# One stored transfer per task for the bands, and the loads of k issued by ScalarE

## The chip, the cores and the metric

The kernel runs on one core of a Trainium2 chip. The time is the device time of one launch, in microseconds, and lower is better. Engines are named as in the profile: PE is TensorE, DVE VectorE, ACT ScalarE, POOL GpSimd, SP SyncE, which only issues transfers here.

## The reference

x is 8 tiles of 512 tokens by 128. Each tile goes through half an expert layer, attention, and half an expert layer again, each behind a layer norm:

```python
x = x + 0.5 * ffn(layernorm(x))        # 8 experts, 128 -> 512 -> 128, summed over all experts
x = x + attention(layernorm(x))
x = x + 0.5 * ffn(layernorm(x))
# ffn:  h = silu(x @ wg) * (x @ wu);  acc + h @ wd
# attention, 16 heads of 8: q, k rotated;  rel = rel_emb[clip(j - i, -32, 32) + 32]
scores = q @ k.T / sqrt(8) + einsum(q, rel)          # causal
attn = softmax(scores)
ctx = attn @ v + einsum('bhqk,qkd->bhqd', attn, rel)
out = ctx @ w_o.T
```

The relative term differs from a constant only within 32 positions left of the diagonal, so it is computed on a band: per query 32 probabilities.

## The kernel before

**Passes.** PASSES names 16 expert passes: A of tile t (first expert layer) and B of tile t (second one), of CH = 32 chunks each (8 experts, 4 blocks of 128 hidden units). A chunk n is gate (three matmuls of 512 columns, L814 to L818), tanh on ACT (L965), gated on DVE (L1100), up (three matmuls, L747 to L749), product on DVE (L1106), hi, a cast on ACT (L971), lo, the rest on POOL (L1274), down (L833, L834) and down_lo (L841) on PE. At a pass's end acc copies the sum to xn (L982), sum_turned turns it on PE (L753), sum adds it on DVE (L1155). A layer norm is ln_stats on DVE (L1068, L1073), ln_rstd, four small steps on POOL (L1258 to L1263), ln_scaled on ACT into the same buffer xn (L948), ln_turned on PE (L759), ln_hi on ACT (L995) and ln_lo on DVE (L1078).

**Attention** of a tile runs beside the passes of other tiles, in four groups of four heads, and a group in 11 tasks: one for the first 128 queries (4 heads), two for the second 128 (2 heads each), four each for the third and fourth (1 head). A task is scores on PE (L896), near, largest and shift on DVE (L1203, L1208, L1214), exp on ACT (L1016), p_hi, the f16 part, on ACT (L1027, L1029), and the rest by p_lo on DVE (L1221) or p_lent on POOL (L1289). All of it lies in probs, a ring of PB = 4 buffers: first the high parts of the task's heads, then the low parts. Two kinds of transfers leave from there, both issued by SyncE: p_turn (L712), a DMA transpose into probs_t, for values on PE (L914); and store_band (L697, L700), which writes the last 160 columns to a scratch in memory, from which load_band on ACT's queue (L1055) reads 32 diagonal columns per query. A two-head task takes two store transfers (L697), one for each part, since in the scratch all high parts of four heads come before all low parts. band_turn (L729) transposes the bands, band_values on PE (L923) multiplies by rel_c, once for the high and once for the low parts, outproj (L932) closes the group, and attention_sum (L1245) adds it.

**k and q.** Per tile project (L747 to L749) makes q and k in four steps, rotate turns them on DVE (the last step L1185), qk_hi and qk_lo split them in the buffer rope, qk_store (L666) writes them to memory. load_q (L1035) is one transfer on ACT's queue per group; load_k (L722) is four transfers of 64 KB per group on SyncE's queue, one for each head of k_pad. v_add (L1190) writes v into the low half of rope and so waits until k is stored. load_k waits for the stores of k and for the scores of the group two before.

**Order.** Each engine's program is one list, made while the kernel is built by a planner: `step(engine, takes, time, name, arg, ...)` gives every step an engine, a duration, a wanted time and what it follows; the wanted time is shifted by a table LATER, a number for each kind of step. The planner takes, at every moment, on the engine that can start first, the open step with the earliest start. So a changed table, duration or engine of one step moves steps on all engines.

Of the kernel before, what the change touches and what calls it, by code (L numbers as in the profile page):

```python
# [8 lines left out]
def macaron_kernel(nc, x_d, wg_d, wu_d, wd_d, watt_d, wo_d, rel_g_d, rel_g0_d, rel_c_d, rel_c0_d,  # L9
                   rel_k0_d, rel_v0_d, cos_d, sin_d, window_d, ident_d, lanes_d, out_d):  # L10
    F32 = mybir.dt.float32
    F32R = mybir.dt.float32r
    F16 = mybir.dt.float16
    BF16 = mybir.dt.bfloat16
# [10 lines left out]
    H = 16  # L25
# [21 lines left out]
    VS = 3  # L47
    VD = VS * DH + 2
# [47 lines left out]
    def quad_of(k):  # L96
# [11 lines left out]
    LATER = {"acc": -1137.9, "attention_sum": -218.9, "band_turn": -615.6, "band_values": -1012.4, "constants":  # L108
             913.7, "denominators": 112.4, "down": 37.6, "down_lo": -171.0, "exp0": -214.2, "exp1": -230.3, "exp2": -211.3,
             "exp3": -141.2, "fill": 311.2, "gate": 24.9, "gated": 150.9, "hi": -147.6, "largest0": -149.5, "largest1":  # L110
             -244.5, "largest2": -479.1, "largest3": -133.8, "ln_hi": -663.8, "ln_lo": -640.3, "ln_rstd": 807.9,
             "ln_scaled": -89.2, "ln_stats": -1456.5, "ln_turned": -297.3, "lo": -278.6, "load_band0": -814.8,
# [5 lines left out]
             "p_turn3": 46.7, "prepare_hi": -414.6, "prepare_lo": 27.6, "product": 137.5, "project": -422.1, "project_v":  # L118
             50.0, "qk_hi": -1536.9, "qk_lo": -982.9, "qk_store": -451.6, "qrel": 24.3, "qrel_copy": -357.1, "qrel_store":
# [284 lines left out]
    with ctx:  # L404
# [167 lines left out]
        for k in range(B * NK):  # L572
            counted[k % PB] += 2 if HEADS[TASKS[k % NK][1]] == 2 else 1
            stores.append(16 * counted[k % PB])
# [795 lines left out]
```

## Time and profile before

| | us |
|---|---|
| median of 3 runs | 1328.59 (1327.34 to 1330.45) |
| the profiled execution | 1326.2 |
| its span on the core | 1324.4 |
| PE busy | 1303.8 |
| DVE busy | 1212.5 |
| POOL busy | 1061.2 |
| ACT busy | 1060.4 |

The profile is one execution. Busy times count computing instructions only; an engine's DMA issues, waits and branches don't count, though an issue holds the queue of the engine that makes it. A group of rows of one line gives count, shortest, median and longest duration. A wait is put down to the event that came last.

### The profile page before, as it was taken

What the parts mean: (1) busy time and instruction counts of PE and PEld (TensorE: products, weight loads), DVE (VectorE), ACT (ScalarE), POOL (GpSimd) and SP (SyncE); (2) the same over time, 40 slices, a digit from 0 to 9 for tenths busy, and PEclk for the clock granted to TensorE, in tenths of its full rate; (3) what the DMA queues carried; (4) which work ended last, traced back from release to release, by engine and by line L of the source; (5) the groups of instructions that cost most, each with busy time, mean ns of one, the idle gap of its engine ahead of it and who ended that gap; (6) DMA issues with size and microseconds to landing.
All of it is one profiled execution on the core that took longest, in us unless ns stands there. A gap on an engine that the chain in (4) does not pass through costs nothing. (4 is left out here: it accounts for less than half of the span.)

```text
span 1324.4 us, 28469 instructions
## 1 busy us (share of the span) xinstructions
PE 1303.8 (98%) x8334; PEld 1051.1 (79%) x8334; DVE 1212.5 (92%) x2613; ACT 1060.4 (80%) x2097; POOL 1061.2 (80%) x979
## 2 busy tenths in 40 slices
PE   8999999999999999999999999999999989999998
PEld 6888888777777788878888888887888867888887
DVE  7887999999999999999999999999999989998665
ACT  6765888878888888888887888888888778887565
POOL 7977888879778887887877977889778787788565
PEclk9999999999999999999999999999999999999999
DMA  6404899999999999999999999999999999997100
GB/s 200 154 1 129 150 228 222 200 219 230 202 233 201 196 197 196 248 184 217 203 209 229 193 223 209 190 231 205 208 201 206 188 220 214 203 176 144 13 9 8
DMA packets 718555, 241.39 MB, mean 182 GB/s; under 512 B 652480, under 2 KB 681920, under 8 KB 718400
## 3 DMA queue, kind: packets, MB, share of 16 engines
q1 hardware_dynamic: 562240, 180.84, 69.7%
q10 hardware_dynamic: 156160, 58.74, 22.0%
q8 instruction: 66, 1.08, 0.3%
q14 instruction: 89, 0.73, 0.2%
HBM read 77.33 MB, written 69.86 MB: 111 GB/s over the span
## 5 line engine op out<-in xcount | busy, mean ns | idle before, releaser
L1274 POOL TENSOR_TENSOR hid_lo<-hid,hid_hi 128x512 fp32r<-128x512 f32 x511 | 658.8, 1296 | 190.2 <-ACT hid_hi L971 101.6
L971 ACT CAST hid_hi<-hid 128x512 fp32r<-128x512 f32 x512 | 317.1, 626 | 94.9 <-PE acc L834 56.8
L1100 DVE SCALAR_TENSOR_TENSOR hid<-hid,work 128x512 f32<-128x512 f32 x512 | 344.5, 679 | 44.6 <-ACT hid L965 44.0
L965 ACT ACTIVATE hid<-work 128x512 f32<-128x512 f32 x512 | 305.9, 600 | 96.5 <-PE work L818 62.1
L1106 DVE TENSOR_TENSOR hid<-hid,work 128x512 f32<-128x512 f32 x512 | 345.8, 680 | 21.7 <-PE work L749 19.5
L1289 POOL TENSOR_TENSOR probs<-exps,probs 128x512 f16<-128x512 f32 (+1 forms) x288 | 304.2, 1061 | 45.1 <-ACT probs L1027 44.2
L1208 DVE TENSOR_REDUCE negmax<-work 128x1 f32<-128x384 f32 (+3 forms) x352 | 220.1, 632 | 0.7
L1016 ACT ACTIVATE exps<-work,negmax_shifted 128x512 f32<-128x512 f32 (+2 forms) x320 | 188.3, 602 | 36.8 <-DVE negmax_shifted L1214 26.1
L747 PE MATMUL work<-xt,wu 128*128 128x512 f32 x512 | 204.9, 400 | 4.0 <-DVE rope L1190 1.5
L841 PE MATMUL acc<-hid_lo,wd 128*128 128x512 f32 x512 | 204.9, 406 | 0.1
L833 PE MATMUL acc<-hid_hi,wd 128*128 128x512 f32 x512 | 203.7, 398 | 0.5 <-ACT hid_hi L971 0.5
L814 PE MATMUL work<-xt,wg 128*128 128x512 f32 x512 | 202.7, 396 | 1.3 <-ACT xt L958 0.8
L815 PE MATMUL work<-xt,wg 128*128 128x512 f32 x512 | 200.2, 391 | 0.0
L818 PE MATMUL work<-xt,wg 128*128 128x512 f32 x512 | 200.1, 391 | 0.0
L749 PE MATMUL work<-xt,wu 128*128 128x512 f32 x512 | 200.1, 391 | 0.0
L834 PE MATMUL acc<-hid_hi,wd 128*128 128x512 f32 x512 | 200.0, 391 | 0.0
L748 PE MATMUL work<-xt,wu 128*128 128x512 f32 x512 | 199.9, 390 | 0.0
L1027 ACT ACTIVATE probs<-exps 128x512 f16<-128x512 f32 (+1 forms) x288 | 167.7, 586 | 12.1 <-issue 4.0
L1203 DVE TENSOR_TENSOR work<-work,rel_win 128x160 f32<-128x160 f32 (+2 forms) x352 | 163.2, 471 | 13.3 <-PE work L896 10.9
L896 PE MATMUL work<-k_pad,qq 128*128 128x512 f32 (+1 forms) x352 | 131.6, 384 | 0.3 <-ACT exps L1016 0.2
L747 PEld LDWEIGHTS work<-xt,wu 128*128 128x128 f32 x512 | 96.2, 188 | 29.1 <-DVE hid L1106 2.1
L814 PEld LDWEIGHTS work<-xt,wg 128*128 128x128 f32 x512 | 96.2, 188 | 23.4 <-DVE hid L1100 1.2
(104 smaller groups left out, 1734.9 us busy)
## 6 DMA issues: line engine op xcount, KB each, us to landing
rel_win<-rel_window_scratch ACTq DMA_DIRECT2D x128, 320.0 KB, 4.0
prob_window_scratch<-probs SPq DMA_DIRECT2D x384, 80.0 KB, 3.3
q_scratch<-rope SPq DMA_DIRECT2D x16, 512.0 KB, 4.2
qq<-q_scratch ACTq DMA_DIRECT2D x32, 256.0 KB, 4.0
k_scratch<-rope SPq DMA_DIRECT2D x16, 512.0 KB, 4.5
rel_window_scratch<-g_s SPq DMA_DIRECT2D x32, 256.0 KB, 3.5
k_pad<-k_scratch SPq DMA_DIRECT2D x128, 64.0 KB, 3.8
prob_window_scratch<-probs SPq DMA_DIRECT2D x32, 256.0 KB, 3.8
```

The lines of the kernel that those rows point to most:

```text
L747: pe.matmul(out, w_hi, m_hi, start=start, stop=False)
L814: pe.matmul(bank[:, :], wg[:, HI, e, cols], x_hi, start=True, stop=False)
L815: pe.matmul(bank[:, :], wg[:, LO, e, cols], x_hi, start=False, stop=False)
L833: pe.matmul(acc[:, :], wd[:, HI, e, cols], hid_hi[:, arg % HH, :], start=(k == 0), stop=False)
L841: pe.matmul(acc[:, :], wd[:, HI, e, cols], hid_lo[:, arg % HH, :], start=False, stop=(k == CH - 1)).then_inc(s_dlo, 1)
L965: act.activation(hid[:, arg % HB, :], work[bank_of["gate", arg]][:, :], ACT.Tanh, scale=0.5).then_inc(s_tanh, 1)
L971: act.copy(hid_hi[:, arg % HH, :], hid[:, arg % HB, :]).then_inc(s_hhi, 1)
L1100: dve.scalar_tensor_tensor(out=hid[:, arg % HB, :], in0=hid[:, arg % HB, :], scalar=1.0, in1=work[bank_of["gate", arg]][:, :], op0=ALU.add ...
L1106: dve.tensor_tensor(hid[:, arg % HB, :], hid[:, arg % HB, :], work[bank_of["up", arg]][:, :], ALU.mult).then_inc(s_hid, 1)
L1208: dve.tensor_reduce(negmax[:, place:place + len(places)], heads, AX.X, ALU.min).then_inc(s_max, 1)
L1274: pool.tensor_tensor(hid_lo[:, arg % HH, :], hid[:, arg % HB, :], hid_hi[:, arg % HH, :].bitcast(F32), ALU.subtract).then_inc(s_hlo, 1)
L1289: pool.tensor_tensor(probs[:, arg % PB, cols:2 * cols], exp_of(arg)[:, 0:cols], probs[:, arg % PB, 0:cols], ALU.subtract).then_inc(s_plent, 1)
```

## The change

Three things are changed.

1. In probs and in the scratch the parts are laid out by pairs of heads: for each pair the two high parts, then the two low parts (a one-head task has its high and its low part, as before). The store of a task is then one transfer in all cases. band_values multiplies by pairs in place of parts: rel_c gets two empty slots (6 in place of 4) and each of the two matmuls takes its window of four slots. by_pairs gives p_hi, p_lo and p_lent their views, and values finds its blocks by the new place.
2. load_k is a step of ACT in place of SP; its waits and its four transfers are the same.
3. LATER has other numbers, and the planner's duration of store_band is 0.62 for all.

The buffer for a small marker (settled) moves into lanes, and the function lower_part is renamed restpart.

```diff
     SCALE = 2.0 ** 14
     VS = 3
+    SLOTS = HQ + 2
+    RC = SLOTS * R
...
-            step("SP", 1.8, first - 14, "load_k", gg, ("qk_store", (t, 1)), ("zero", 7),
+            step("ACT", 1.8, first - 14, "load_k", gg, ("qk_store", (t, 1)), ("zero", 7),
...
-            step("SP", 1.2 if HEADS[i] == 2 else 0.62, due[k] + 2.5, "store_band", k, lower(k),
+            step("SP", 0.62, due[k] + 2.5, "store_band", k, lower(k),
...
-             -131.5, "scores3": 23.8, "shift1": -584.8, "shift2": -672.7, "shift3": -980.9, "split_hi": 63.7, "split_lo":
+             -258.7, "scores3": 20.3, "shift1": -386.5, "shift2": -453.1, "shift3": -684.5, "split_hi": -52.3, "split_lo":
...
-        rel_c = sb("rel_c", [P, HQ, R // DH, DH], BF16)
+        rel_c = sb("rel_c", [P, SLOTS, R // DH, DH], BF16)
...
+        def by_pairs(k):
+
+            quad, i, places, keys = task(k)
+            pairs = max(len(places) // 2, 1)
+            both = probs[:, k % PB, 0:2 * len(places) * keys].rearrange("p (u h c) -> p u h c", u=pairs, h=2)
+            whole = exp_of(k)[:, 0:len(places) * keys].rearrange("p (u c) -> p u c", u=pairs)
+            return both[:, :, HI, :], both[:, :, LO, :], whole
...
-                    base = (quad % (2 * NT) * 2 * HQ + places[0]) * TILE + lo
-                    if n == 2:
-                        for part in (HI, LO):
-                            sp.dma_start(bass.AP(pwin_t, base + part * HQ * TILE, [[W, P], [TILE, n], [1, W - lo]]),
-                                         near[:, part, :, :]).then_inc(stored(arg)[0], 16)
-                    else:
-                        sp.dma_start(bass.AP(pwin_t, base, [[W, P], [HQ * TILE // n, 2 * n], [1, W - lo]]),
-                                     near.rearrange("p h n k -> p (h n) k")).then_inc(stored(arg)[0], 16)
+                    first = quad % (2 * NT) * 2 * HQ + places[0] // 2 * 4 + places[0] % 2
+                    sp.dma_start(bass.AP(pwin_t, first * TILE + lo,
+                                         [[W, P], [TILE if n > 1 else 2 * TILE, 2 * n], [1, W - lo]]),
+                                 heads[:, :, keys - W + lo:keys]).then_inc(stored(arg)[0], 16)
...
-                    for part in (HI, LO):
+                    for pair in range(2):
                         done = pe.matmul(ctx_p[:, :].rearrange("p (i q) -> p i q", i=NT),
-                                         rel_c[:, :, :, :].rearrange("p a s d -> p (a s d)"), band_t[:, :, part, :],
-                                         start=False, stop=(part == LO), skip_group_check=True)
+                                         rel_c[:, 2 - 2 * pair:SLOTS - 2 * pair, :, :].rearrange("p a s d -> p (a s d)"),
+                                         band_t[:, :, pair, :], start=False, stop=(pair == 1), skip_group_check=True)
...
+                if name == "load_k":
+                    t, g = arg // HG, arg % HG
+                    act.wait_ge(s_qst[1], 32 * (t + 1))
+                    if arg < 2:
+                        act.wait_ge(s_zero, 8)
+                    else:
+                        act.wait_ge(s_sc, GK * (arg - 1))
+                    for a in range(HQ):
+                        act.dma_start(k_pad[a:P:HQ, arg % 2, a, :].bitcast(F32),
+                                     bass.AP(k_t, t % VB * 4 * P * L + g * L + a * HG * L,
+                                             [[H * L, 4 * DH], [1, L]])).then_inc(s_kld[arg % 2], 16)
```

Three places of the engines' lists show what the new numbers do. Names are tile<-tiles; line numbers are each kernel's own, and in the changed kernel L808 to L812 is gate, L741 to L743 up, L827 and L828 down, L835 down_lo, L927 outproj, L747 sum_turned, L753 ln_turned.

The first place is PE's list at the last hand-over, from the last output projection of attention (L932) to the first gate of the last pass. Before, 30 wide matmuls lie between it and the turn of the norm (the first and the last of them are shown):

```order
4985 L932 MATMUL work<-wo,ctx_s 128x128 x4
4986 L841 MATMUL acc<-hid_lo,wd 128x512
4987 L814 MATMUL work<-xt,wg 128x512
...
5014 L834 MATMUL acc<-hid_hi,wd 128x512
5015 L841 MATMUL acc<-hid_lo,wd 128x512
5016 L759 MATMUL work<-ident,xn 128x128 x4
5017 L833 MATMUL acc<-hid_hi,wd 128x512
5018 L834 MATMUL acc<-hid_hi,wd 128x512
5019 L841 MATMUL acc<-hid_lo,wd 128x512
5020 L833 MATMUL acc<-hid_hi,wd 128x512
5021 L834 MATMUL acc<-hid_hi,wd 128x512
5022 L814 MATMUL work<-xt,wg 128x512
```

In the changed kernel the same stretch is:

```order
4999 L927 MATMUL work<-wo,ctx_s 128x128 x4
5000 L835 MATMUL acc<-hid_lo,wd 128x512
5001 L827 MATMUL acc<-hid_hi,wd 128x512
5002 L828 MATMUL acc<-hid_hi,wd 128x512
5003 L827 MATMUL acc<-hid_hi,wd 128x512
5004 L828 MATMUL acc<-hid_hi,wd 128x512
5005 L835 MATMUL acc<-hid_lo,wd 128x512
5006 L827 MATMUL acc<-hid_hi,wd 128x512
5007 L828 MATMUL acc<-hid_hi,wd 128x512
5008 L835 MATMUL acc<-hid_lo,wd 128x512 x2
5009 L747 MATMUL work<-ident,xn 128x128 x4
5010 L753 MATMUL work<-ident,xn 128x128 x4
5011 L808 MATMUL work<-xt,wg 128x512
```

Ten wide matmuls and the turn of pass 14's sum now lie between the projection and the turn of the norm, and the gate follows the turn at once.

The second place is SyncE's list from the time when the loads of k of tile 7 start. Before:

```order
701 L722 DMA k_pad<-k_scratch 32x512 x4
702 L700 DMA prob_window_scratch<-probs 128x2x160
703 L712 DMA_TRANSPOSE probs_t<-probs 128x6x128
704 L700 DMA prob_window_scratch<-probs 128x2x160
705 L712 DMA_TRANSPOSE probs_t<-probs 128x8x128
706 L722 DMA k_pad<-k_scratch 32x512 x4
...
711 L700 DMA prob_window_scratch<-probs 128x8x128
712 L712 DMA_TRANSPOSE probs_t<-probs 128x8x128
713 L697 DMA prob_window_scratch<-probs 128x2x160 x2
714 L712 DMA_TRANSPOSE probs_t<-probs 128x8x128
715 L697 DMA prob_window_scratch<-probs 128x2x160 x2
```

In the changed kernel, with the store of k of tile 7 (L677) in the middle:

```order
662 L704 DMA prob_window_scratch<-probs 128x2x160
663 L704 DMA prob_window_scratch<-probs 128x8x128
664 L717 DMA_TRANSPOSE probs_t<-probs 128x8x128
665 L677 DMA k_scratch<-rope 128x2x512 x2
666 L689 DMA rel_window_scratch<-g_s 128x4x128
667 L717 DMA_TRANSPOSE probs_t<-probs 128x8x128
668 L704 DMA prob_window_scratch<-probs 128x4x160
669 L717 DMA_TRANSPOSE probs_t<-probs 128x8x128
670 L704 DMA prob_window_scratch<-probs 128x4x160
671 L717 DMA_TRANSPOSE probs_t<-probs 128x8x128
```

The loads of k are gone from the list, and a two-head task has one store of 128x4x160 where it had two of 128x2x160.

The third place is ACT's list where the first load of k of tile 7 is now. Before, the list has there, behind the load of q:

```order
1780 L1035 DMA qq<-q_scratch 128x512
1781 L1016 ACTIVATE exps<-work,negmax_shifted 128x512
1782 L971 CAST hid_hi<-hid 128x512
1783 L1055 DMA bands<-prob_window_scratch 128x8x32
1784 L1027 ACTIVATE probs<-exps 128x512
1785 L965 ACTIVATE hid<-work 128x512
```

In the changed kernel:

```order
1665 L966 CAST hid_hi<-hid 128x512
1666 L1021 ACTIVATE probs<-exps 128x384
1667 L1049 DMA rel_win<-rel_window_scratch 128x640
1668 L1038 DMA k_pad<-k_scratch 32x512 x4
1669 L960 ACTIVATE hid<-work 128x512 x2
1670 L1011 ACTIVATE exps<-work,negmax_shifted 128x384
1671 L966 CAST hid_hi<-hid 128x512
```

Five issues in a row stand ahead of the next tanh (L960).

## Rows read from the trace of the kernel before

**Rows 1.** Busy time, share of the span and instructions of each engine.

```profile
PE 1303.8 (98%) x8334; PEld 1051.1 (79%) x8334; DVE 1212.5 (92%) x2613; ACT 1060.4 (80%) x2097; POOL 1061.2 (80%) x979
```

**Rows 2.** Stretches: length; busy PE, PEld, DVE, ACT, POOL; clock; DMA share; GB/s.

```profile
0.00:50.00 50.00, 44.75 (x195) 36.53 (x196) 37.74 (x74) 34.93 (x64) 42.44 (x40) 1.00 0.61 197
...
250.00:430.00 180.00, 174.54 (x1167) 136.41 (x1165) 170.66 (x381) 148.62 (x300) 145.31 (x138) 1.00 1.10 214
430.00:880.00 450.00, 449.54 (x3036) 363.26 (x3035) 434.40 (x968) 380.71 (x766) 372.00 (x345) 1.00 1.09 208
880.00:1120.00 240.00, 234.68 (x1646) 188.43 (x1645) 229.48 (x514) 199.48 (x402) 195.82 (x185) 1.00 1.07 208
...
1260.00:1324.40 64.40, 60.69 (x268) 49.53 (x266) 39.55 (x61) 35.71 (x60) 38.43 (x30) 1.00 0.02 7
```

**Rows 3.** Waits of PE, 140 to 1245 us: total, times, longest.

```profile
PE ctx_p L914 <- DMA probs_t<-probs: 2.9, 4, 1.8
PE ctx_p L923 <- DMA band_t<-bands: 1.8, 2, 1.0
PE work L747 <- DVE rope L1190: 1.5, 1, 1.5
PE work L747 <- ACT exps L1016: 1.1, 1, 1.1
```

**Rows 4.** DMA issues by line: duration in ns, shortest/median/longest, first and last start.

```profile
L712 SPq DMA_TRANSPOSE probs_t<-probs x352: 1209/1256/4925, 140.7 to 1223.0; - x176
L697 SPq DMA_DIRECT2D prob_window_scratch<-probs x128: 359/484/1555, 142.1 to 1199.9; - x128
L722 SPq DMA_DIRECT2D k_pad<-k_scratch x128: 448/587/2072, 123.0 to 1151.1; - x128
L1035 ACTq DMA_DIRECT2D qq<-q_scratch x32: 326/350/434, 111.0 to 1147.2; - x32
```

**Rows 5.** Timeline of SP, DVE and PE, 381 to 391 us: start, duration.

```profile
381.45 1.04 SPq L666 DMA_DIRECT2D k_scratch<-rope  x2
...
389.76 0.69 DVE L1190 TENSOR_TENSOR rope<-work,rel_v 128x512 f32<-128x512 f32 x1 [2.53 <-DMA k_scratch<-rope]
...
390.51 0.50 PE L747 MATMUL work<-xt,wu 128*128 128x512 f32 x1 [1.54 <-DVE rope L1190]
```

**Rows 6.** Timeline of ACT, SP and PE, 1076 to 1086 us.

```profile
1076.96 0.63 ACT L1027 ACTIVATE probs<-exps 128x512 f16<-128x512 f32 x1 [2.07 <-DMA probs_t<-probs]
...
1076.21 2.45 SPq L722 DMA_DIRECT2D k_pad<-k_scratch  x4
1078.76 0.53 SPq L700 DMA_DIRECT2D prob_window_scratch<-probs  x1
1079.39 1.23 SPq L712 DMA_TRANSPOSE probs_t<-probs  x1
...
1085.88 0.85 PE L914 MATMUL ctx_p<-probs_t,values 128*25 128x128 f16 x48 [1.84 <-DMA probs_t<-probs]
```

**Rows 7.** Timeline of PE, DVE, POOL and ACT, 1243 to 1253 us.

```profile
1243.69 0.40 PE L834 MATMUL acc<-hid_hi,wd 128*128 128x512 f32 x1
1243.92 1.05 PE L932 MATMUL work<-wo,ctx_s 128*128 128x128 f32 x8
1244.73 0.47 PE L841 MATMUL acc<-hid_lo,wd 128*128 128x512 f32 x1
...
1245.02 0.69 DVE L1245 TENSOR_TENSOR x<-work,x 128x512 f32<-128x512 f32 x1 [0.33 <-PE work L932]
...
1248.49 0.20 POOL L1263 TENSOR_TENSOR shift<-mean_neg,rstd 128x4 f32<-128x4 f32 x1
1248.64 1.29 POOL L1274 TENSOR_TENSOR hid_lo<-hid,hid_hi 128x512 fp32r<-128x512 f32 x1
...
1249.71 1.65 ACT L948 ACTIVATE xn<-x,shift,rstd 128x128 f32<-128x128 f32 x4
...
1252.30 0.59 ACT L995 CAST xt<-work 128x512 fp32r<-128x512 f32 x1
```

More of the change, by code:

```diff
@@ L104, in macaron_kernel @@
     LANDS = {"PE": 0.35, "ACT": 0.35, "DVE": 0.35, "POOL": 0.35, "SP": 2.6}
[L108 to L112, printed above, removed]
[5 rows of a table removed]
-             "p_turn3": 46.7, "prepare_hi": -414.6, "prepare_lo": 27.6, "product": 137.5, "project": -422.1, "project_v":
-             50.0, "qk_hi": -1536.9, "qk_lo": -982.9, "qk_store": -451.6, "qrel": 24.3, "qrel_copy": -357.1, "qrel_store":
[3 rows of a table removed]
-             "store_band3": -469.7, "sum": 611.7, "sum_turned": -628.3, "tanh": -270.2, "up": 27.8, "v_add": 678.4,
-             "v_split": -14.5, "values": -612.1, "zero": 1284.8}
+    LATER = {"acc": -1094.5, "attention_sum": -283.2, "band_turn": -812.0, "band_values": -638.2, "constants":
+             868.8, "denominators": 94.4, "down": 40.5, "down_lo": -282.6, "exp0": -235.8, "exp1": -327.3, "exp2": -134.0,
+             "exp3": -89.0, "fill": 634.3, "gate": 24.8, "gated": 153.4, "hi": -141.5, "largest0": -189.7, "largest1":
+             -271.4, "largest2": -570.6, "largest3": -154.1, "ln_hi": -575.5, "ln_lo": -738.8, "ln_rstd": 736.8,
+             "ln_scaled": -86.0, "ln_stats": -1530.5, "ln_turned": -296.9, "lo": -290.8, "load_band0": -897.7,
[5 rows of a table added]
+             "p_turn3": 383.9, "prepare_hi": -585.7, "prepare_lo": -29.1, "product": 95.7, "project": -277.9, "project_v":
+             58.0, "qk_hi": -1705.2, "qk_lo": -829.6, "qk_store": -477.8, "qrel": 31.4, "qrel_copy": -373.9, "qrel_store":
[3 rows of a table added]
+             "store_band3": -576.7, "sum": 697.1, "sum_turned": -679.8, "tanh": -378.9, "up": 28.5, "v_add": 696.4,
+             "v_split": 178.1, "values": -526.5, "zero": 1337.8}
     OF_TASK = ("scores", "near", "largest", "shift", "exp", "p_hi", "p_lo", "p_lent", "p_turn", "store_band")
@@ L451, in macaron_kernel @@
         ident = sb("ident", [P, P])
-        lanes = sb("lanes", [P, 2])
+        lanes = sb("lanes", [P, 3])
         stats = sb("stats", [P, NT, 6])
@@ L1019, in _ @@
                     quad, i, places, keys = task(arg)
-                    cols = len(places) * keys
                     act.wait_ge(s_exp, unit(quad, places[-1]) + 1)
@@ L1286, in _ @@
                     quad, i, places, keys = task(arg)
-                    cols = len(places) * keys
                     pool.wait_ge(s_phi, arg + 1)
-                    pool.tensor_tensor(probs[:, arg % PB, cols:2 * cols], exp_of(arg)[:, 0:cols],
-                                       probs[:, arg % PB, 0:cols], ALU.subtract).then_inc(s_plent, 1)
+                    upper, rest, whole = by_pairs(arg)
+                    pool.tensor_tensor(rest, whole, upper, ALU.subtract).then_inc(s_plent, 1)
                 if name == "v_split":
@@ L1333 @@
         rel_g0[a, :, :, :, a] = rel[0][:, None]
-    rel_c, rel_c0 = np.zeros((HQ, R, HQ, 4, DH), rel.dtype), np.zeros((HQ, R, HQ, 4, DH), rel.dtype)
-    for a in range(HQ):
-        rel_c[a, :, a, 0:3, :] = rel[1:R + 1][:, None, :]
-        rel_c0[a, :, a, 0:3, :] = rel[0]
+    rel_c, rel_c0 = np.zeros((2, 2, R, HQ + 2, 4, DH), rel.dtype), np.zeros((2, 2, R, HQ + 2, 4, DH), rel.dtype)
+    for a in range(2):
+        rel_c[:, a, :, 2 + a, 0:3, :] = rel[1:R + 1][:, None, :]
+        rel_c0[:, a, :, 2 + a, 0:3, :] = rel[0]
     w_o = np.asarray(inputs["L0_attn_w_o"])
```

55 lines of the change are left out of this document (20 added, 35 removed), and 14 rows, old and new, of the table LATER.

## The prediction

> **What bounds the kernel now.** I read the profile in this order. First the busy shares: TensorE (PE) is busy for 1303.8 of 1324.4 us, 98% [rows 1]. A busy PE is no proof that PE sets the end, so the second view is the table of stretches [rows 2]: it says where PE's 20.6 us of idle time lie. They lie in four places: the start (5.25 us), the stretch 250 to 430 us (180.00 - 174.54 = 5.46), the stretch 880 to 1120 us (240.00 - 234.68 = 5.32) and the end (64.40 - 60.69 = 3.71). The 450 us between 430 and 880 lose 0.46 us in all. The granted clock is 1.00 in every row, so the clock plays no part. The same table shows what stands next in line: from 430 to 880 VectorE (DVE) is busy for 434.40 of 450 us (96.5%) and ScalarE (ACT) for 380.71 (85%). So PE's own work sets the time, DVE has almost no room to catch up after a hole, and ACT has some.
>
> Third, the waits of PE in the attention part [rows 3]: transposes that land late (2.9 us), band transposes (1.8), one wait of 1.5 on DVE's L1190 and one of 1.1 on ACT's exp. Fourth, the stretches where they happen. Until 390.51 us PE stands for 1.54 us because DVE stands for 2.53 us: L1190 overwrites the buffer from which k is being stored and waits for that store. The store was issued at 381.45 behind transposes on SyncE's queue [rows 5]. Until 1076.96 ACT stands for 2.07 us waiting for a transpose, and the 1.1 us of PE on ACT's exp follow from it; until 1085.88 PE stands 1.84 us for a transpose that SyncE issued at 1079.39, after a store (1078.76) which itself followed four loads of k (1076.21 to 1078.66) [rows 6]. So the two clusters are delays of SyncE's queue and its transfers, and the change takes work from just this queue.
>
> **What the change can't move.** The matmuls are the same in number and width: band_values still runs two matmuls of 512 columns per group, with another slice of rel_c as weights; scores, values and the expert matmuls keep their shapes. Wide matmuls (512 columns) follow each other at 0.23 us, start to start [rows 7], and will in the changed kernel. Bytes stay too: a two-head task stores the same 160 KB, in one transfer for two. The regrouping by pairs changes the address pattern of p_hi and the low part only for tile 0 of each group (32 tasks, two runs of 256 columns for one of 512); a tenth more of 0.6 us on 32 instructions would be 2 us of ACT, off the path, and I take 0. The longer constants and subtractions happen before 110 us, where PE loses nothing [rows 2]. I take 0 for the start and the end.
>
> **Part 1, SyncE's queue is relieved.** The loads of k leave it: 128 issues x 0.587 us = 75 us. The second store of the 64 two-head tasks goes: 64 x 0.484 = 31 us. Together 106 us of queue time. What stays is mostly 352 transposes x 1.256 = 442 us [rows 4]. A queue that is not the bound gives back only lateness, so the gain is capped by what PE loses in the two clusters: 5.46 + 5.32 = 10.8 us. I don't take all of it. First, part of the lateness is not issue time: the store of k at 381.45 took over 7 us to land [rows 5], and the transfers' bytes stay. Second, the new order puts some consumers closer. Between the last step of k's rotation and L1190 DVE has in the old order 28, 33 and 23 instructions for tiles 2, 3 and 7; in the new one 22, 35 and 27. Tile 3 and tile 7 get more time, tile 2 less, so the wait at L1190 can come back at tile 2. Third, from the last projection of k of tile 7 to its first scores the new PE order has some 9 us more work (32 us for 23, counting 0.23 us per wide matmul), which gives the second cluster more room. Bounds: all 10.8 us gone, or none. I take a bit under half, -5 us (from -10.8 to 0), since of the waits named in [rows 3], 2.9 + 1.8 + 1.5 us are of this kind and each shortens by one or two issues of 0.5 us rather than vanishing.
>
> A rule speaks against this part. What the rows show first: a group's four loads of k hold SyncE for 2.45 us [rows 6], more than any single wait of PE in [rows 3], so issuing is not small here. The Trainium skill (DMA: Bandwidth & Descriptors, section Issuing engines are not separate DMA queues) says that issuing from several engines saves only the sequencer's time, which is "usually small relative to the DMA itself", since all run on the same 16 DMA engines. By it part 1 would be near 0 instead of -5.
>
> **Part 2, ScalarE issues the loads of k.** 32 times four issues in a row stand ahead of ACT's work: what is queued behind them is tanh of the next chunk (L965), the cast L971 and the exp of the next task, and DVE and then PE wait for those. The trace has no such load on ACT. Nearest rows: ACT's own load of q issues in 0.350 us (4 x 0.350 = 1.4 us); the same load on SyncE in 0.587 (4 x 0.587 = 2.35) [rows 4]. The issue runs while ACT's last instruction still computes (about 0.6 us), so the hole is 0.8 to 1.75 us. Its waits (k stored, the scores of two groups before) are satisfied well before where it now stands: in the new order PE has 10 us of work or more between the load of k and the group's first scores. What does a hole of ACT cost PE? The ACT hole of 2.07 us in [rows 6] cost PE the 1.1 us of [rows 3], in a crowded place. From 430 to 880 us ACT stands idle many times and PE loses 0.46 us in all [rows 2]. Bounds: 0 for all 32, or 32 x 0.4 = 13 us. I take +2 us, near the low end, as most of the loads lie in stretches like the latter.
>
> **Part 3, the new order at the last hand-over.** The last pass (B of tile 7) needs the layer norm of tile 7, which needs the last attention output. The order of before keeps 30 wide matmuls between the last L932 and the turn of the norm, and five more before the first gate; PE loses nothing there. In the new order only ten wide matmuls, the turn of pass 14's sum and the turn of the norm stand between, and then the gate. The chain itself, by [rows 7]: L932 ends at about 1244.8 (the next matmul starts at 1244.73); the sum on DVE ends at 1245.71, and after the statistics and POOL's four steps the shift is ready at 1248.69. Then ACT's scaling 1.65 us (in before it came an us late, at 1249.71, as nothing hurried), so 1250.4; the last transposes and the start of the high cast about 0.3 later, 1250.7; the cast 0.59, 1251.3; the gate at 1251.4, which is 6.6 us after L932. PE's work between is 10 x 0.23, twice four turns of 128 columns (2 x 0.4, by the 0.81 us of L932's eight), and 0.1 for the change of form = 3.2 us, and the gate's third matmul waits some 0.3 us more for the low part. That gives 6.6 - 3.2 + 0.3 = 3.7 us. It is more if the low parts of the last three chunks queue on POOL (1.29 us each, ahead of its norm steps and needed for pass 14's sum, which must leave the shared buffer xn before the scaling starts): then up to 4.8. I take +4.2 us (3.6 to 4.8), as the three chunks do stand close together there. The rest of PE's work is the same, so nothing later gives it back.
>
> **Sum.** On the profiled execution (span 1324.4, time 1326.2): -5 + 2 + 4.2 = +1.2 us. The profiled run lies 2.4 us below the median of the three timed runs (1328.59), an ordinary spread of this kernel (1327.34 to 1330.45), so I set the change on the median: 1328.59 + 1.2 = 1329.8 us. A measurement of this kernel can tell about 0.2%, 2.7 us, from no change; so faster means under 1325.9, slower over 1331.3.
>
> **Rivals.**
> - *SyncE's lateness was nearly all of it.* -9 of the 10.8 us, ACT's loads cost 0.5, the hand-over 4.2: -4.3, that is 1324.3 us. For it: both clusters lead back to that queue [rows 5, 6]. Against: the landing times, and 450 us in which the same queue is as full and PE loses nothing. Chance 0.24.
> - *No relief, only the hand-over.* The clusters come from DMA transfers and crowded norms rather than issue; part 1 gives 0.5, ACT costs 1.5, the hand-over 4.2: +5.2, 1333.8 us, slower. It decides from where part 1 is worth under 3.5 us. Chance 0.22. The rule of the Trainium skill quoted above would have it go this way.
> - *ACT's holes reach PE through DVE.* DVE, 96.5% busy, can't catch up: a hole of ACT of over 1 us becomes a hole of DVE, and 32 x 0.3 = 9.6 us of PE, with -4 for part 1 and 4.2: +9.8, 1338.4 us. It decides from about 0.15 us per load. For it: half of ACT's hole of 2.07 us arrived at PE [rows 3, 6]. Against: ACT's 15% of room. Chance 0.14.
> - *The forecast*, relief and costs within 2.7 us of each other: 0.40, with its own range 1326 to 1331.3.
>
> From these: faster 0.25, within 0.2% 0.40, slower 0.35. The range reaches into both neighbours, from 1323 to 1337 us; outside stay the full relief with no cost of ACT, and the worse half of ACT's case.
>
> **What would show it.** Right: a PE wait of 3.6 to 4.8 us in one or two pieces just ahead of the last pass's first gate, at about 1245 to 1255 us, with the chain L932, sum, statistics, POOL, scaling in front of it; SyncE's queue some 100 us emptier; the idle time of PE from 250 to 430 and 880 to 1120 us down from 10.8 to about 6; four DMA issues of 0.35 to 0.6 us each on ACT, followed by an idle ACT of about 1 us, but seldom an idle PE. Wrong: no stall at the hand-over (then the chain is shorter than I add it up); clusters as large as before, or new ones at L1190 of tile 2; idle time of PE spread through 430 to 880 us right behind the loads of k, which would be the third rival.

## The result, and the profile after

The changed kernel takes 1349.5 us (median of 4 runs, 1344.1 to 1353.7) beside 1329.5 us for the kernel before, run on the same chip (1327.3 to 1332.7). The ratio is 1.0152, with a 95% interval from 1.0118 to 1.0186. So it is slower by 20 us, where 1329.8 us was forecast with a range up to 1337. The profiled execution has a span of 1346.4 us where [rows 1] belongs to one of 1324.4: 22.0 us more.

The busy line of the page, which answers to [rows 1]:

```profile
PE 1318.9 (98%) x8334; PEld 1052.4 (78%) x8334; DVE 1215.3 (90%) x2613; ACT 1049.7 (78%) x2097; POOL 1061.1 (79%) x979
```

The instructions are as many as before. PE's busy time is 15 us longer with the same matmuls: it takes in the short delays between one matmul and the next, so most of the loss doesn't show as idle time in it. The stretches, which answer to [rows 2] (same columns):

```profile
250.00:430.00 180.00, 177.53 (x1189) 141.24 (x1188) 169.10 (x377) 146.20 (x297) 143.56 (x135) 1.00 1.06 201
430.00:880.00 450.00, 444.33 (x3012) 351.76 (x3010) 426.70 (x953) 372.18 (x756) 363.68 (x338) 1.00 1.08 206
880.00:1120.00 240.00, 235.44 (x1571) 187.36 (x1560) 226.53 (x497) 193.36 (x392) 191.41 (x179) 0.99 1.03 204
```

PE's idle time from 250 to 430 us fell from 5.46 to 2.47 us, and from 880 to 1120 us from 5.32 to 4.56. But from 430 to 880 us, where it had been 0.46, it is now 5.67, and DVE does less there (426.70 for 434.40). The waits of PE from 140 to 1262 us, which answer to [rows 3], are short and of many kinds; none is over 1.7 us:

```profile
PE work L890 <- ACT exps L1011: 2.4, 3, 1.6
PE ctx_p L909 <- DMA probs_t<-probs: 2.4, 3, 1.2
PE acc L835 <- POOL hid_lo L1274: 1.7, 4, 0.6
PE acc L827 <- ACT hid_hi L966: 1.2, 3, 0.8
PE work L808 <- DVE rope L1192: 1.2, 1, 1.2
```

To see the rest I set the start of every matmul against the sum of the matmuls before it, taken at their usual spacing, and read how far the wall clock had run ahead. The table gives this lag in us, by the work that PE has done so far (left column). The usual spacing is a choice that moves all columns together by a few us, so only differences between them are read. e12, e4 and e9 are experiments that are told below.

| PE's work, us | before | after | e12 | e4 | e9 |
|---|---|---|---|---|---|
| 150 | 9.7 | 12.4 | 12.8 | 10.3 | 9.3 |
| 400 | 25.4 | 26.5 | 26.3 | 24.8 | 28.8 |
| 650 | 32.4 | 39.0 | 36.9 | 36.4 | 36.3 |
| 900 | 39.8 | 54.4 | 49.6 | 48.7 | 52.1 |
| 1200 | 51.8 | 68.7 | 60.0 | 58.5 | 61.7 |
| 1250 | 52.1 | 74.1 | 66.5 | 63.6 | 64.4 |

Up to 400 us of work the changed kernel loses 1.1 us against before (2.7 at the start, of which 1.6 come back). Between 400 and 1200 it loses 15.8 us more than before, a little in most steps of 50 us, and in the one step from 1200 to 1250, the last hand-over, 5.4 us where before loses 0.3.

**The hand-over.** PE, DVE, POOL and ACT in the timeline, which answer to [rows 7] (start, duration, and in brackets the idle time before):

```profile
1266.89 1.05 PE L927 MATMUL work<-wo,ctx_s 128*128 128x128 f32 x8
...
1267.98 0.69 DVE L1245 TENSOR_TENSOR x<-work,x 128x512 f32<-128x512 f32 x1 [1.28 <-PE work L927]
...
1271.07 0.63 PE L747 MATMUL work<-ident,xn 128*128 128x128 f32 x4 [0.78 <-ACT xn L977]
1271.47 0.20 POOL L1263 TENSOR_TENSOR shift<-mean_neg,rstd 128x4 f32<-128x4 f32 x1
...
1271.81 1.65 ACT L943 ACTIVATE xn<-x,shift,rstd 128x128 f32<-128x128 f32 x4 [0.89 <-PE work L747]
...
1272.45 1.39 PE L753 MATMUL work<-ident,xn 128*128 128x128 f32 x4 [0.76 <-ACT xn L943]
...
1274.52 0.72 PE L808 MATMUL work<-xt,wg 128*128 128x512 f32 x1 [0.68 <-ACT xt L990]
1275.03 0.63 PE L809 MATMUL work<-xt,wg 128*128 128x512 f32 x1
1275.46 0.63 PE L812 MATMUL work<-xt,wg 128*128 128x512 f32 x1
...
1278.02 0.41 PE L743 MATMUL work<-xt,wu 128*128 128x512 f32 x1
```

From the end of the projection (L927, about 1267.9) to the gate (1274.52) it is 6.6 us, the figure of the forecast's chain (6.8 if the end is read from the start of the next matmul, 1267.70, as the forecast did), and the ten wide matmuls and two turns don't fill it. Two chains end together here: the norm's shift is ready at 1271.67, and the scaling (L943) starts at 1271.81, when the turn of pass 14's sum (L747, to 1271.70) has also left the buffer xn.

**ScalarE's row of issues.** The line of the loads of k, which answers to L722 in [rows 4], and two of the 32 places where they stand, in ACT's timeline:

```profile
L1038 ACTq DMA_DIRECT2D k_pad<-k_scratch x128: 456/617/1487, 127.4 to 1185.7; - x128
```

```profile
760.14 0.58 ACT L960 ACTIVATE hid<-work 128x512 f32<-128x512 f32 x1
760.72 0.34 ACTq L1027 DMA_DIRECT2D qq<-q_scratch  x1
761.15 2.41 ACTq L1038 DMA_DIRECT2D k_pad<-k_scratch  x4
763.76 0.79 ACTq L1058 DMA_DIRECT2D bands<-prob_window_scratch  x1
764.66 0.62 ACT L966 CAST hid_hi<-hid 128x512 fp32r<-128x512 f32 x1 [3.94 <-DMA prob_window_scratch<-probs]
...
1087.93 3.45 ACTq L1038 DMA_DIRECT2D k_pad<-k_scratch  x4
1091.76 1.09 ACT L960 ACTIVATE hid<-work 128x512 f32<-128x512 f32 x2 [3.67 <-issue]
```

A load issues in 0.617 us. The row of four takes 2.39 to 3.82 us (median 2.50), its first load 0.467 and each later one 0.62 us (medians). In the first place a load of q and one of bands stand beside it, and ACT computes nothing for 3.94 us; in the second the row alone takes 3.45 us, and ACT stands for 3.67. The hole isn't the row's length, though, since ACT's queue can run ahead of its computing. At 208.02 us the whole row issues while instructions that stand ahead of it in the list still compute (L1011 at 208.39 and 208.75, L998 at 209.10, L966 at 209.58), and the hole is 0.63 us:

```profile
208.02 0.47 ACTq L1038 DMA_DIRECT2D k_pad<-k_scratch  x1
...
209.58 0.66 ACT L966 CAST hid_hi<-hid 128x512 fp32r<-128x512 f32 x1
209.81 0.61 ACTq L1038 DMA_DIRECT2D k_pad<-k_scratch  x1
210.88 0.62 ACT L994 CAST rope<-rope 128x512 fp32r<-128x512 f32 x1 [0.63 <-DVE rope L1187]
```

In 16 of the 32 rows at least one such instruction starts within the row. The holes are 0.63 to 3.94 us. DVE and PE behind the row at 1087.93:

```profile
1092.39 1.28 DVE L1103 SCALAR_TENSOR_TENSOR hid<-hid,work 128x512 f32<-128x512 f32 x2 [0.94 <-ACT hid L960]
...
1091.42 0.40 PE L743 MATMUL work<-xt,wu 128*128 128x512 f32 x1
1093.37 0.44 PE L890 MATMUL work<-k_pad,qq 128*128 128x384 f32 x1 [1.55 <-ACT exps L1011]
```

ACT stands, DVE has no tanh to multiply, the next exp comes late, and PE stands for 1.55 us. In most places PE sees only some tenths of this, later. So the candidates are: the length of the row on ACT; the queue that issues it; the order of the lists, which also changed everywhere; and the hand-over.

### The profile page after: what moved, and what is told of

Read it like the earlier page. It is cut to its first block and busy times, and to the rows that moved or that the text cites. A ratio compares the mean times of both kernels' runs of the same rounds, so it can differ in the third digit from the quotient of the medians.

```text
span 1346.4 us, 28405 instructions
## 1 busy us (share of the span) xinstructions
PE 1318.9 (98%) x8334; PEld 1052.4 (78%) x8334; DVE 1215.3 (90%) x2613; ACT 1049.7 (78%) x2097; POOL 1061.1 (79%) x979
## 3 DMA queue, kind: packets, MB, share of 16 engines
q10 hardware_dynamic: 162304, 67.14, 24.8%
## 5 line engine op out<-in xcount | busy, mean ns | idle before, releaser
L960 ACT ACTIVATE hid<-work 128x512 f32<-128x512 f32 x512 | 307.2, 605 | 125.8 <-PE work L812 55.8
L966 ACT CAST hid_hi<-hid 128x512 fp32r<-128x512 f32 x512 | 316.4, 631 | 78.7 <-DVE hid L1109 44.6
L1011 ACT ACTIVATE exps<-work,negmax_shifted 128x512 f32<-128x512 f32 (+2 forms) x320 | 187.7, 609 | 36.4 <-DVE negmax_shifted L1216 23.1
L808 PE MATMUL work<-xt,wg 128*128 128x512 f32 x512 | 206.0, 402 | 4.4 <-DVE rope L1192 1.2
L835 PE MATMUL acc<-hid_lo,wd 128*128 128x512 f32 x512 | 207.3, 412 | 1.8 <-POOL hid_lo L1274 1.7
L827 PE MATMUL acc<-hid_hi,wd 128*128 128x512 f32 x512 | 204.3, 399 | 2.2 <-ACT hid_hi L966 1.2
L741 PE MATMUL work<-xt,wu 128*128 128x512 f32 x512 | 204.8, 400 | 1.4 <-DVE hid L1109 0.7
L812 PE MATMUL work<-xt,wg 128*128 128x512 f32 x512 | 201.3, 393 | 0.0
L743 PE MATMUL work<-xt,wu 128*128 128x512 f32 x512 | 200.7, 392 | 0.0
L828 PE MATMUL acc<-hid_hi,wd 128*128 128x512 f32 x512 | 199.9, 390 | 0.0
L1021 ACT ACTIVATE probs<-exps 128x512 f16<-128x512 f32 (+1 forms) x288 | 166.6, 588 | 14.1 <-DMA prob_window_scratch<-probs 4.3
L808 PEld LDWEIGHTS work<-xt,wg 128*128 128x128 f32 x512 | 97.0, 189 | 30.1 <-DVE hid L1103 3.9
L741 PEld LDWEIGHTS work<-xt,wu 128*128 128x128 f32 x512 | 96.6, 189 | 27.4 <-DVE hid L1109 3.9
```

What stands on the lines that cost most here:

```text
L741: pe.matmul(out, w_hi, m_hi, start=start, stop=False)
L808: pe.matmul(bank[:, :], wg[:, HI, e, cols], x_hi, start=True, stop=False)
L812: pe.matmul(bank[:, :], wg[:, HI, e, cols], x_lo, start=False, stop=True).then_inc(s_gate, 1)
L827: pe.matmul(acc[:, :], wd[:, HI, e, cols], hid_hi[:, arg % HH, :], start=(k == 0), stop=False)
L835: pe.matmul(acc[:, :], wd[:, HI, e, cols], hid_lo[:, arg % HH, :], start=False, stop=(k == CH - 1)).then_inc(s_dlo, 1)
L960: act.activation(hid[:, arg % HB, :], work[bank_of["gate", arg]][:, :], ACT.Tanh, scale=0.5).then_inc(s_tanh, 1)
```

## Experiments

All ratios are to the kernel before on the same chip, which had medians of 1327.7 to 1328.7 us. The experiments ran on four chips, so where two runs with different medians of before are compared, the ratios are the safer measure. e4, e7, e8, e10, e14 and e16 spread the loads.

**e1, the stores alone.** The lists of before, with the new layout and one store per task.

```diff
-            step("ACT", 1.8, first - 14, "load_k", ...
+            step("SP", 1.8, first - 14, "load_k", ...
-            step("SP", 0.62, due[k] + 2.5, "store_band", ...
+            step("SP", 1.2 if HEADS[i] == 2 else 0.62, due[k] + 2.5, "store_band", ...
```

(to the changed kernel; LATER as before, and the four loads under SyncE.)

> The order, the table and the queue of load_k are those of before; only the layout by pairs and the single store are changed. If the layout or the single store (its 160 KB land in 3.9 us where 80 KB landed in 3.3) costs the 20 us, this is near 1345 us. Theory (the loads of k on ScalarE cost it): this is within 3 us of before, 1326 to 1331, with some 31 us less of SyncE's issue time, and PE's idle time not above 21 us.

Measured: 1329.9 us, ratio 1.0016 (0.9993 to 1.0038). Layout and store change nothing that can be told, and SyncE's queue with 64 issues less gives nothing back. PE's two clusters didn't shrink either: in the profiled execution (1334.9 us, the upper end of e1's runs) PE is idle for 3.35 and 8.61 us in the two stretches, 12.0 in place of 10.8.

```profile
250.00:430.00 180.00, 176.65 (x1179) 138.89 (x1178) 173.72 (x389) 150.71 (x303) 148.29 (x142) 1.00 1.08 216
880.00:1120.00 240.00, 231.39 (x1569) 186.02 (x1568) 222.92 (x494) 194.52 (x391) 189.39 (x177) 0.98 1.05 200
```

**e2, the loads on ScalarE, lists otherwise as in e1.** The block of load_k moves from SyncE's loop to ScalarE's.

> As e1, and the four loads of k are issued by ScalarE at the same places of the planner's common list; all lists of PE, DVE and POOL are those of before. Theory of ScalarE's holes: four issues in a row take 2.4 us or more there (0.46 + 3 x 0.62), holes of 1.5 to 3.5 us follow 32 times, and PE loses 0.3 to 0.6 us each: 10 to 19 us over e1, 1338 to 1348 us. Theory of the new order (the table LATER and the last hand-over): no more than 3 us over e1.

Measured: 1372.5 us, 1.0329 (1.0312 to 1.0347), 43 us over e1, where 10 to 19 were expected. The waits of PE, 140 to 1245 us:

```profile
PE work L808 <- ACT exps L1011: 12.6, 10, 1.8
PE work L890 <- ACT exps L1011: 7.2, 10, 1.6
```

The longest are all for ACT's exp. In lists that hadn't been laid for it, a row costs over 1 us (43 / 32).

**e3, the changed kernel with the loads back on SyncE**, at the same places of the common order.

> The changed kernel with its order, but the loads of k issued by SyncE at the same places of the common list. Theory of ScalarE's holes: the 10 to 15 us that they cost go, and the stall of 5 us at the last hand-over stays: 1333 to 1338 us, ratio to before 1.003 to 1.007. Theory of the new order: it stays near 1349 us.

Measured: 1357.5 us, 1.0234 (1.0203 to 1.0266): 8 us slower than with the loads on ACT, and outside both expectations. PE waits for SyncE's transfers instead (140 to 1245 us):

```profile
PE ctx_p L920 <- DMA probs_t<-probs: 5.5, 3, 2.9
PE ctx_p L929 <- DMA band_t<-bands: 4.9, 4, 2.5
PE work L819 <- DVE rope L1192: 4.0, 1, 4.0
```

So in either order the queue for which the lists were laid is the better one: which engine issues can't be priced apart from the order.

**e4, the changed kernel, the row spread.** Nothing else moves.

```diff
-                    for a in range(HQ):
-                        act.dma_start(k_pad[a:P:HQ, arg % 2, a, :]...)
+                    to_load.extend((arg, a) for a in range(HQ))
...
             for name, arg in order:
+                if to_load and name in ("tanh", "hi", "p_hi", "exp"):
+                    x, a = to_load.pop(0)
+                    act.dma_start(k_pad[a:P:HQ, x % 2, a, :]...)
```

> The changed kernel, but ScalarE issues the four loads of k one at a time, each ahead of one of its next four steps, in place of four in a row. If it is the length of the row that makes the hole: single issues take about 0.46 us (as the first of a row does now, against 0.62 for the next three) and lie under the running instruction, so ScalarE's holes shrink to those of load_q, and the time falls by 8 to 14 us, to 1335 to 1341. If it is the issue time as such, wherever it lies, it falls by no more than the 128 x 0.15 us saved, spread: under 3 us.

Measured: 1336.6 us, 1.0063 (1.0049 to 1.0076), 12.9 us faster than the changed kernel (11.8 by the ratios). ACT's timeline around the place that stood for 3.94 us above:

```profile
758.09 0.61 ACTq L960 DMA_DIRECT2D k_pad<-k_scratch  x1
758.82 0.62 ACT L972 CAST hid_hi<-hid 128x512 fp32r<-128x512 f32 x1 [1.80 <-DVE hid L1112]
758.84 0.51 ACTq L960 DMA_DIRECT2D k_pad<-k_scratch  x1
759.47 0.69 ACT L1017 ACTIVATE exps<-work,negmax_shifted 128x512 f32<-128x512 f32 x1
759.49 0.51 ACTq L960 DMA_DIRECT2D k_pad<-k_scratch  x1
```

An issue (0.51 us) runs while the instruction ahead of it computes (0.62 to 0.69 us), and is hidden. A row of 2.5 us needs several such instructions waiting ahead of it, as at 208.02 us above, and mostly they aren't there. In the lag table e4 loses 33.7 us between 400 and 1200 us of work, before 26.4 and after 42.2. The step of the hand-over (1200 to 1250) stays, 5.1 us.

**e5 to e8, other plans.** The planner's table and load_k's entry are varied; single stores in all. e5 is the old LATER with the loads planned and issued on ACT, e7 the same spread, e8 spread with a planned duration of 0.45, and e6 the new LATER with the loads planned and issued on SyncE.

```diff
-    LATER = {... "load_k": 314.5, ...}
+    LATER = {... "load_k": 214.3, ...}
```

(e5, e7, e8: the whole old table.)

```diff
-            step("ACT", 1.8, first - 14, "load_k", ...
+            step("SP", 1.8, first - 14, "load_k", ...
```

(e6; in e8 "ACT", 0.45.)

> The changed kernel with the table LATER of before, all else as changed: load_k is a step of ScalarE of 1.8 us, issued four in a row. Its PE list keeps 7.0 us of work between the last output projection and the turn of the last norm (the changed kernel 2.7, before 6.8). If the loads on ScalarE are the cause, it is as slow as the changed kernel less the stall of 5 us at the hand-over, or slower, since no table was fitted to it: 1343 to 1352 us. If the new table is the cause, it is near before: 1326 to 1334 us.

> The new table LATER with load_k planned and issued on SyncE, single stores. Its PE list has 0.0 us of work between the last output projection and the turn of the last norm. If the loads on ScalarE are the cause, only the hand-over costs: 6 to 8 us by its chain of 6.6 us, 1334 to 1340 us. If the new table itself is the cause, it is as slow as the changed kernel or slower: 1345 to 1360 us.

> As e5, but the four loads are issued one at a time ahead of ScalarE's next steps. Theory of the row: it takes some 13 us off e5, as it did from the changed kernel (1349.5 to 1336.6). With the hand-over filled (7.0 us of work) it should then be at or below before: 1325 to 1333 us.

> As e7, but the planner is told 0.45 us for load_k in place of 1.8, which is nearer to what a spread group hides; hand-over 8.2 us of work. A candidate for the fastest: 1322 to 1332 us. If single issues still cost ScalarE as much as a row, the plan is now too tight and it is slower than e7 by 5 us or more.

Measured: e5 1363.8 us (1.0252, 1.0222 to 1.0282), e6 1350.7 (1.0159, 1.0122 to 1.0196), e7 1355.0 (1.0203, 1.0176 to 1.0230), e8 1353.7 (1.0198, 1.0177 to 1.0218). e5, e7 and e8 lie outside everything that was expected, by 12 to 22 us; of e6 the second expectation held, that for the new table: without any load of k on ACT it is as slow as the changed kernel. Spreading gave 9 us here too (e5, e7; the intervals just touch). All four are some 20 us or more over e1, on either queue: in these runs a table was good only for the plan that it was made for. The hand-over's step is 1.5, 10.1, 1.5 and 0.1 us, so it belongs to the order, not to the loads.

**e9, a new order and nothing else.** One number of e1:

```diff
-            step("SP", 1.2 if HEADS[i] == 2 else 0.62, due[k] + 2.5, "store_band", ...
+            step("SP", 0.62, due[k] + 2.5, "store_band", ...
```

> The kernel of before with single stores and the old table, loads of k on SyncE; one number differs from e1: the planner's duration of the store of a two-head task, 0.62 in place of 1.2. The planner then makes another order on all engines (some 8100 of 5300 + 5300 rows of PE's list stand elsewhere). Theory 1, the order of before is a fitted one and any other costs by itself, whatever queue issues the loads of k: some 1345 to 1358 us. Theory 2, only the new table or the move of the loads to ScalarE costs: within 4 us of e1, 1326 to 1334 us.

Measured: 1340.0 us, 1.0077 (1.0051 to 1.0102). It fell between the two expectations: the re-plan by itself costs 10 us (8 by the ratios), less than in e5 to e8. Its lag comes in a few lumps (8.7 us between 350 and 400 us of work, where before loses about 5; 7.6 between 850 and 900, where before loses about 2.5), where bands or casts are late:

```profile
PE ctx_p L929 <- DMA band_t<-bands: 8.2, 3, 4.0
PE acc L838 <- ACT hid_hi L977: 3.4, 5, 1.3
```

In both lumps the granted clock was at its lower level, 0.50, for 6.8 us from 396.9 and for 3.4 us from 912.4. At half the rate that is at most 5 us of the loss, so a part of the price of a new order here is the clock that follows its stalls. The hand-over's step is 2.7 us.

**e10 and e11, the dose in the order of e1.** e10 is e2 spread as in e4. In e11 SyncE issues two of the four loads and ScalarE the other two:

```diff
-                    for a in range(HQ):
-                        sp.dma_start(...)
+                    for a in range(2):
+                        sp.dma_start(...)
...
+                    for a in range(2, HQ):
+                        act.dma_start(...)
```

> The order of before with single stores; the loads of k are issued by ScalarE at the places where e2 issues four in a row, but one at a time, ahead of ScalarE's next four steps. e1 (SyncE) took 1329.9 us, e2 (four in a row on ScalarE) 1372.5. Theory 1, what costs is that a row of four holds ScalarE for 2.3 to 3.8 us at once: spread loads should give back most of the 43 us, 1330 to 1342 us. Theory 2, ScalarE has no room for the issue time at all (128 x 0.5 = 64 us): 1360 us or more.

> The order of before with single stores; of a group's four loads of k SyncE issues two and ScalarE two, at the same places of the common list. Holding ScalarE for two issues is about 1.1 us in place of 2.3. Theory 1, a hole costs only from a certain length on, which the work queued between the engines covers: well under half of e2's 43 us, 1331 to 1343 us. Theory 2, the cost is in proportion to the issue time: about 1351 us.

Measured: e10 1339.3 us (1.0082, 1.0054 to 1.0110), e11 1336.6 (1.0058, 1.0034 to 1.0082). Above e1 a row of two (1.17 us, median) costs 7 us and a row of four (2.42 us) 43 us; four spread ones cost 9 us. The intervals of e1 and e11 leave the 7 uncertain by some 4 us, so double the length costs at least four times as much. In these lists a row of about 1 us is mostly covered, and one of over 2 us isn't; and 128 single issues on ACT aren't free.

**e12, the row shortened.** The changed kernel with one address pattern changed:

```diff
-                        act.dma_start(k_pad[a:P:HQ, arg % 2, a, :].bitcast(F32),
+                        act.dma_start(k_pad[32 * a:32 * a + 32, arg % 2, a, :].bitcast(F32),
```

> The changed kernel, but the four loads of k of a group write partitions 32a to 32a+31 in place of every fourth one, so that scores multiply the wrong rows of k; sizes, sources and numbers of transfers are the same. Theory 1, the issue time of 0.62 us behind another issue is that of the queue and not of the pattern of partitions: 0.6 to 0.65 us each and 1345 to 1353 us. Theory 2, the scattered partitions make the issue long: 0.35 us each, as the load of q, and 1338 to 1343 us.

Its scores multiply the wrong rows of k, so it doesn't compute the reference; only its time is used.

Measured: 1340.1 us, 1.0077 (1.0047 to 1.0107), 9 us less than the changed kernel.

```profile
L1038 ACTq DMA_DIRECT2D k_pad<-k_scratch x128: 324/448/1620, 127.9 to 1176.7; - x128
```

An issue takes 0.448 us in place of 0.617, the row 2.11 in place of 2.50 (medians). The time is in the second range, and the issue time does depend on the partitions written, though it didn't fall to 0.35. With the lists unchanged, a row that is 0.4 us shorter gives some three quarters of what spreading gives, and its lag runs beside that of e4 up to the hand-over.

**e13 to e16, the short row with q ordered alike.** For scores to multiply matching rows, q's must be ordered by head as well:

```diff
                                  bass.AP(q_t, t % VB * 4 * P * L + g * L,
-                                         [[HG * L, P], [1, L]])...
+                                         [[HG * L, HQ], [H * L, 4 * DH], [1, L]])...
```

and constants are permuted. e13 is the changed kernel so, e14 is e13 spread, e15 is e1 so, e16 is e10 so.

> The changed kernel with the rows of q and k of a group ordered by head (partition 32a + c in place of 4c + a), so that each load of k writes 32 neighbouring partitions; constants of the relative term are permuted to match, the result is the same as that of before. Theory 1, the row of issues on ScalarE costs by its length: issues of 0.45 us in place of 0.62, a row of 2.1 us, 1338 to 1342 us as e12. Theory 2, e12 was faster by accident of its data or of wrong products: 1347 to 1352 us.

> As e13, with the four loads issued one at a time ahead of ScalarE's next four steps, as in e4. Theory 1, after spreading a single issue is covered and its length is nothing: as e4, 1335 to 1338 us. Theory 2, cost in proportion to issue time: single issues of 0.34 us in place of 0.505 save 21 us of ScalarE's queue and some 3 to 5 us more, 1331 to 1334 us; the hand-over keeps 5 us above before in both.

> The order of before, single stores, loads of k on SyncE, with contiguous partitions. SyncE's issues of k should take 0.45 us in place of 0.587, 17 us of its queue less, on top of the 31 us of the single stores. Theory 1, PE's two clusters come from SyncE's lateness (part 1 of the prediction): a gain, 1320 to 1326 us. Theory 2, the clusters are not of issue time, as e1 showed for the stores: within 3 us of e1, 1327 to 1332 us.

> As e15, but the loads of k issued by ScalarE one at a time, as in e10 (1339.3 us). If ScalarE's issue time costs, 0.34 in place of 0.51 us each gives back part of the 9.4 us that e10 lies above e1: 1332 to 1336 us. If it is their place in the order that costs, 1337 to 1341 us.

Measured: 1371.6, 1364.1, 1376.7 and 1389.5 us (1.0344, 1.0275, 1.0379, 1.0469; the widest interval is 1.0295 to 1.0392). All missed by some 20 us or more, because the load of q changed: e13 differs from e12 in this load and in constants alone, and takes 31 us more. From e15, the line of that load:

```profile
L1038 ACTq DMA_DIRECT2D qq<-q_scratch x32: 531/532/1096, 110.8 to 1186.0; - x32
```

and two waits of PE, 140 to 1262 us:

```profile
PE ctx_p L920 <- DMA probs_t<-probs: 19.0, 14, 3.6
PE work L891 <- DMA qq<-q_scratch: 5.0, 4, 2.1
```

In e1 they are 343 ns (median), 6.9 us and 0.3 us. The last packet of q lands 5.95 us after the start of the issue in e15 and 3.2 in e1 (medians), and a transfer of q signals its semaphore 5 times in place of 16. The Trainium skill (DMA: Bandwidth & Descriptors, section Why a DMA increments its semaphore by 16 and not by 1) says that the sizes of both patterns' slowest dimensions set how many of the 16 engines a transfer uses, and that the share of the unused ones is signalled at once. With a slowest dimension of 4 beside one of 128 that is four engines and five signals; the trace has the five signals. So e13 to e16 don't speak on the row. That the transposes are late because they queue behind q is read from the waits, not tested. The medians of e13 and e14 differ by 7.5 us, again for spreading, but their intervals overlap. I found no version that beats the kernel before.

## Why the prediction was wrong, step by step

**Part 3, the hand-over: right in its chain, and in its size with some luck.** 4.2 us were forecast (3.6 to 4.8); the step measures 5.1 more than before, after a chain of 6.6 us as added up. But the forecast let the clock play no part, and it does: from 1274.52 to 1278.02 eight wide matmuls take 3.5 us where 8 x 0.23 = 1.8. Without these 1.7 us the step would be 3.4, just under the lower bound. The 5.1 are read from the traces; no run fills the hand-over and leaves all else.

**Part 2, ScalarE issues the loads: the mis-sized term.** +2 us were taken, from 0 to 13. e4 puts the price of the row at 12.9 us by medians (10.5 between the profiled spans), 0.4 us per row of four, which is the far end of the bounds. Two steps failed. The price of an issue was read from ACT's load of q (0.350) and SyncE's of k (0.587), and the hole as 0.8 to 1.75 us; the issue took 0.617, and in 20 of the 32 rows ACT computes nothing for 2.0 to 3.9 us; in four of the five longest (3.4 us and more) a load of q, of bands or of a window stands beside the row. And the value was taken near the low end since PE lost 0.46 us in the calm stretch. That stretch was calm with ACT holes of half a us on average, the longest 1.7; it said nothing on holes of 2 us and more, of which the changed kernel has nine there. ACT's waits from 430 to 880 us before, the row with the longest one (total, times, longest):

```profile
ACT hid L965 <- PE work L818: 23.3, 40, 1.7
```

The sentence that should have decided was in the forecast itself: DVE is busy 96.5% and has almost no room to catch up. The waits of DVE for ACT from 430 to 880 us show it, before and after:

```profile
DVE probs L1221 <- ACT probs L1029: 1.8, 4, 0.6
DVE hid L1100 <- ACT hid L965: 1.6, 3, 0.9
```

```profile
DVE probs L1223 <- ACT probs L1021: 7.7, 9, 1.5
DVE hid L1103 <- ACT hid L960: 6.4, 12, 0.9
```

3.4 us became 14.1; in e4 the same two are 6.6 us and in e12 7.7. The forecast's own sign of being wrong came too: PE's idle time from 430 to 880 us is 5.67 us in place of 0.46. This was the third rival, at the right place and by the right chain, priced at 0.3 us per load; it had a chance of 0.14. Its sum, 1338.4 us, still fell short by 11 us: it counted on 4 us of relief that no run shows, and it had no term for the order.

**Part 1, SyncE relieved: not -5.** For the stores e1 measures nothing. In the changed kernel the clusters did shrink, from 10.8 to 7.0 us, but in e1's fixed lists they are 12.0, so this isn't the relief of 64 issues; and no run took the loads off SyncE without putting them on ACT, so what their removal alone gives stays open. The rule of the Trainium skill that was quoted against this part (DMA: Bandwidth & Descriptors, section Issuing engines are not separate DMA queues) agrees with e1 for the stores. It is no guide for a row on a computing engine: there the row takes 2.50 us where a load lands 4.2 us after the start of its issue (medians), and it was the largest term.

**The order as a whole: a term that was missing.** Only the hand-over was priced. e9 shows that a new order of the same work, with the same queues, can cost 10 us, in lumps at places that no reading of the lists pointed out. In the changed kernel it cost less: e4 lies 8.4 us above before by ratio, some 5 of it the hand-over, so some 3 us are left for all other moves together, the relief among them. The sum of the loss then reads 12 (row) + 5 (hand-over) + 3 (rest) = 20 us. By the profiled executions alone it is 10.5 + 4.8 + 6.7 = 22 us, so the rest is known to a few us only. The rest can't be split into relief and cost from these runs.

## What to carry to other kernels

A transfer issued from a computing engine is cheap if it is one issue behind a computing instruction of at least its length (9 us for 128 of them in e10), and several in a row are mostly a hole for the engines behind (43 us in e2). Price the row, with every other issue that stands in it, against the slack of the next engine, not of the one that issues. When a queue's issues go to a computing engine, spread them. Lists that were laid for one placement lost here in every run that issued the same loads from another queue in a row (e2, e3, e11) or changed a planned time (e9), so a placement is judged only after a new fit, and a new fit only by its own time.

## What the runs showed of the hardware

**Issue time.** The same load of 32 rows takes 0.467 us as first of a row on ACT and 0.62 behind another; spread (e4), 0.505; writing neighbouring partitions in place of every fourth (e12), 0.330 as the first and 0.45 to 0.47 behind. On SyncE it is 0.540 and 0.59 (e1). All are medians. ACT's queue ran up to four computing instructions ahead of its computing (the row at 208.02 us).

**The clock.** The trace of before has a granted clock of 1.00 throughout. In the changed kernel it fell to the lower of its two levels (1.2 in place of 2.4 GHz) for 3.4 us after the stall of 1.55 us at 1093.37, and again in the hand-over, after PE had stood three times for 0.7 to 0.8 us. Windows of the trace (length, busy PE, PEld, DVE, ACT, POOL, clock, DMA share, GB/s):

```profile
1092.00:1095.00 3.00, 1.63 (x5) 1.34 (x6) 2.43 (x5) 3.00 (x7) 1.92 (x3) 0.79 1.29 233
1273.00:1276.00 3.00, 2.21 (x7) 1.36 (x7) 0.69 (x1) 1.05 (x3) 0.00 (x0) 0.77 0.31 87
1276.00:1279.00 3.00, 3.00 (x11) 2.34 (x10) 1.65 (x3) 1.19 (x2) 0.00 (x0) 0.66 0.00 0
```

At the lower level wide matmuls follow each other at 0.43 us (1275.03, 1275.46) in place of 0.23, so a stall of PE can be followed by a second price: 1.7 us in the hand-over. Not every stall is: in before PE stood for 1.54 us until 390.51 and for 1.84 until 1085.88, and the clock stayed at 1.00. Twice that price is under 4 us of the 22, and a run of the changed kernel with a mean clock of 1.00 took 1349.0 us all the same: the clock adds to the loss and doesn't explain it.
